# Local attention of a hybrid kernel: exponentials written back to the scores' PSUM bank and divided out of it, the statistics placed after the token shift has had time to land, and new instruction orders

## The reference

```python
def _layer(x, wqkv, qs, ksc, wo, lg, lb, w1, b1, w2, b2):
    h = shift_token(x)                 # half of the channels come from the token before
    q, k, v = split(h @ wqkv)          # 8 heads of 64
    q = l2norm(q) * qs; k = l2norm(k) * ksc
    q, k = rotary_xpos(q, k)
    o = local_attention(q, k, v)       # windows of 64 tokens, keys of this window and the one before
    x = x + o @ wo
    h = shift_token(x)
    h = layernorm(h) * lg + lb
    a, g = split(h @ w1 + b1)          # hidden width 341
    x = x + (a * gelu(g)) @ w2 + b2
# local_attention: attn = softmax(sim + mask); out = attn @ v
```

## Time and profile before

| | us |
|---|---|
| three runs, median (lowest to highest) | 2002.58 (1999.52 to 2009.76) |
| the profiled execution, own time | 2001.32 |
| its span | 1999.5 |
| PE, DVE, ACT, POOL busy in it | 1614.6, 1371.7, 1116.0, 453.6 |

### The profile page before, as it was taken

The page is one execution under the profiler, slowest core; times in us unless marked ns, Lnnn a source line. Parts: engine busy times, 40 slices in busy tenths (PEclk is TensorE's granted clock), DMA queues, the critical chain, the costliest instruction groups (busy, mean ns, idle before and its releaser), DMA issues.

```text
span 1999.5 us, 31315 instructions
## 1 busy us (share of the span) xinstructions
PE 1614.6 (81%) x9756; PEld 1271.6 (64%) x9787; DVE 1371.7 (69%) x3495; ACT 1116.0 (56%) x2975; POOL 453.6 (23%) x342
## 2 busy tenths in 40 slices
PE   6999989666466787888887899999967788888886
PEld 5888887344354565666666687777735666666665
DVE  4678768788956768677786466456656867768673
ACT  2354454332124777778777644434236777777774
POOL 1210010000003334343343100000023334334340
PEclk9999999676678999999999999989979999999998
DMA  4000000000010000000000000000000000000000
GB/s 136 1 1 0 0 0 1 0 1 0 0 53 1 3 3 1 3 2 3 3 1 3 2 1 0 0 0 0 1 0 3 2 3 1 3 3 2 3 1 24
DMA packets 15110, 13.49 MB, mean 7 GB/s; under 512 B 11286, under 2 KB 14266, under 8 KB 14650
## 3 DMA queue, kind: packets, MB, share of 16 engines
q1 hardware_dynamic: 15034, 12.55, 2.0%
HBM read 9.41 MB, written 1.05 MB: 5 GB/s over the span
## 4 chain that ended last, share of the span: by engine, by line
PE 50%; DVE 25%; issue 10%; ACT 7%; DMA 5%; SPq 1%; DVEq 1%; POOL 1%; ACTq 0%; POOLq 0%
DVE prob L1027 5%; DMA HS<-XH 5%; PE bank L1739 4%; PE bank L1680 4%; PE bank L1751 4%; PE bank L1700 3%; PE bank L1879 3%; DVE arena_ffn L984 3%; PE bank L1772 3%; DVE arena_ffn L980 2%; ACT prob L1437 2%; DVE nmaxF L717 2%; PE bank L1883 2%; PE bank L1691 2%; PE bank L1899 2%
## 5 line engine op out<-in xcount | busy, mean ns | idle before, releaser
L556 POOL TENSOR_TENSOR arena_ffn<-arena_ffn 128x1024 f32<-128x1024 f32 x60 | 140.9, 2348 | 434.2 <-DVE arena_ffn L984 434.2
L552 POOL TENSOR_TENSOR inv<-ssq,mhalf 128x16 f32<-128x16 f32 x64 | 188.3, 2942 | 160.6 <-DVE ssq L993 160.6
L1437 ACT ACTIVATE prob<-bank,nmaxF 128x128 f32<-128x128 f32 x512 | 180.9, 372 | 65.7 <-DVE nmaxF L717 65.7
L1751 PE MATMUL bank<-packF,hT 128*128 128x512 f32 x256 | 146.7, 702 | 74.6 <-DVE arena_ffn L984 66.4
L1027 DVE TENSOR_TENSOR prob<-prob,rdenF 128x512 f32<-128x512 f32 x128 | 180.2, 1408 | 4.4
L1714 PEld LDWEIGHTS bank<-arena_setup 128*128 128x128 f32 x1024 | 145.4, 205 | 18.5 <-issue 10.3
L1367 ACT ACTIVATE prob<-bank,nmax 128x128 f32<-128x128 f32 (+1 forms) x256 | 89.9, 420 | 118.3 <-DVE nmax L717 90.5
L1726 PE MATMUL bank<-ident,prob 128*128 128x128 f32 x512 | 83.5, 286 | 79.7 <-DVE prob L1027 79.7
L1714 PE MATMUL bank<-arena_setup 128*128 128x128 f32 x1024 | 143.9, 287 | 0.0
L540 POOL TENSOR_TENSOR rstd<-var,mhalf 128x2 f32<-128x2 f32 x24 | 17.0, 708 | 518.0 <-DVE var L679 518.0
L1726 PEld LDWEIGHTS bank<-ident,prob 128*128 128x128 f32 x512 | 57.1, 144 | 116.8 <-DVE prob L1027 110.0
(11 more groups left out here) (271 smaller groups left out, 4102.4 us busy)
## 6 DMA issues: line engine op xcount, KB each, us to landing
packF<-in_packF SPq DMA_DIRECT2D x1, 3122.0 KB
arena_history<-in_packG SPq DMA_DIRECT2D x1, 2560.0 KB, 9.8
HS<-XH SPq DMA_DIRECT2D x32, 63.5 KB
X<-in_x_tiled SPq DMA_DIRECT2D x1, 1024.0 KB, 5.0
out_dram<-X SPq DMA_DIRECT2D x8, 128.0 KB, 1.9
arena_setup<-in_const_masks_a SPq DMA_DIRECT2D x1, 512.0 KB, 5.5
HS<-XH SPq DMA_DIRECT2D x32, 0.2 KB
arena_setup<-in_const_rope SPq DMA_DIRECT2D x1, 256.0 KB
```

Source lines behind the costliest of these rows:

```text
L552: pool.tensor_tensor(inv[:, t, :, 0], ssq[:, t, :, 0], mhalf[:, 0:16], ALU.pow).then_inc(sems["inv_ready"], 1)
L556: pool.tensor_tensor(t1[:, t], t1[:, t], t2[:, t], ALU.add).then_inc(sems["rope_sum"], 1)
L1437: ins = act.activation(prob[:, u % 2, c * P:(c + 1) * P], bank[u % F_SCORE_BANKS][:, c * P:(c + 1) * P], ACT.Exp, bias=nmaxF[:, u, c:c + 1 ...
L1751: ins = pe.matmul(bank[banks[m]][:], hT[:, t * P:(t + 1) * P], f_at[f"wqkv{l}"][:, 512 * m:512 * m + 512], start=True, stop=True)
```

## The change

The exponentials are written over the scores in the PSUM bank, and the DVE multiplication reads that bank and writes `prob`. So `local_exp` no longer waits for the transposes of two units before (`pt_ready`); that wait is now `weigh`'s. `local_scores` waits until `weigh` of two units before (`norm_ready`) has read the bank, where it waited for the exponentials (`exp_ready`). The orders of DVE, ACT and PE in a window step are rewritten.

```diff
 # DVE, weigh(u)
                     dve.wait_ge(sems["exp_ready"], v.at("exp_ready", i, u + 1))
                     ch.link(dve.reciprocal(rdenF[:, u], denF[:, u]))
-                    pr = prob[:, u % 2].rearrange("p (c k) -> p c k", k=P)
-                    dve.tensor_tensor(pr, pr, rdenF[:, u].broadcast_to([P, 4, P]), ALU.mult).then_inc(sems["norm_ready"], 1)
+                    dve.wait_ge(sems["pt_ready"], v.at("pt_ready", i, u - 1))
+                    split = lambda a: a.rearrange("p (c k) -> p c k", k=P)
+                    dve.tensor_tensor(split(prob[:, u % 2]), split(bank[u % F_SCORE_BANKS][:]), rdenF[:, u].broadcast_to([P, 4, P]), ALU.mult).then_inc(sems["norm_ready"], 1)
 # DVE, win
+                attn_max(v, i, 0, 4, P, nmaxF, F_SCORE_BANKS)
                 scaled(v, i, 1)
+                if nxt:
+                    rope_part(vn, ni, nl, 0, 0)
+                attn_max(v, i, 1, 4, P, nmaxF, F_SCORE_BANKS)
+                if nxt:
+                    rope_part(vn, ni, nl, 0, 1)
                 if hid:
                     hidden_stats(*hid)
                 if nxt:
-                    rope_part(vn, ni, nl, 0, 0)
-                attn_max(v, i, 0, 4, P, nmaxF, F_SCORE_BANKS)
-                if nxt:
-                    rope_part(vn, ni, nl, 0, 1)
+                    norms(vn, ni, 0, sch)
+                weigh(0)
                 if m:
                     gated(*m)
-                weigh(0)
-                attn_max(v, i, 1, 4, P, nmaxF, F_SCORE_BANKS)
-                if nxt:
-                    norms(vn, ni, 0, sch)
+                weigh(1)
                 attn_max(v, i, 2, 4, P, nmaxF, F_SCORE_BANKS)
                 if nxt:
                     rope_part(vn, ni, nl, 1, 0)
-                weigh(1)
+                if m:
+                    mlp_end(m[0], m[1])
                 attn_max(v, i, 3, 4, P, nmaxF, F_SCORE_BANKS)
                 weigh(2)
-                if m:
-                    mlp_end(m[0], m[1])
...
+                local_residual(v, i, l)
                 if fin:
                     final_stats(m[0], m[1])
-                local_residual(v, i, l)
-                if fin:
                     norm_apply(m[0], m[1])
 # ACT, local_exp(u)
                 act.wait_ge(sems["max_ready"], v.at("max_ready", i, u + 1))
-                act.wait_ge(sems["pt_ready"], v.at("pt_ready", i, u - 1))
                 for c in range(4):
-                    ins = act.activation(prob[:, u % 2, c * P:(c + 1) * P], bank[u % F_SCORE_BANKS][:, c * P:(c + 1) * P],
-                                         ACT.Exp, bias=nmaxF[:, u, c:c + 1], accum_out=denF[:, u, c])
+                    cols = bank[u % F_SCORE_BANKS][:, c * P:(c + 1) * P]
+                    ins = act.activation(cols, cols, ACT.Exp, bias=nmaxF[:, u, c:c + 1], accum_out=denF[:, u, c])
 # ACT, win
                     shifted(vn, ni)
+                if m:
+                    prime(ACT.Gelu)
+                if nxt:
                     squares(vn, ni, 0)
                 if m:
-                    prime(ACT.Gelu)
                     gelus(*m)
                     prime(ACT.Exp, 1)
                 local_exp(v, i, 0)
                 take_qkT(v, i, 1)
+                local_exp(v, i, 1)
                 if nxt:
                     squares(vn, ni, 1)
-                local_exp(v, i, 1)
+                middle_values(v, i)
+                local_exp(v, i, 2)
                 probs_copy(v, i, 0)
-                local_exp(v, i, 2)
-                middle_values(v, i)
                 probs_copy(v, i, 1)
 # PE, local_scores(u)
-                pe.wait_ge(sems["exp_ready"], v.at("exp_ready", i, u - 1))
+                pe.wait_ge(sems["norm_ready"], v.at("norm_ready", i, u - 1))
 # PE, win
                     transpose_x(vn, ni, bank[2])
-                if m:
-                    hidden_gates(*m, 0)
+                local_scores(v, i, 0)
                 if nxt:
                     project_qk(vn, ni, nl, 0)
                 if m:
+                    hidden_gates(*m, 0)
                     pe.wait_ge(sems["down_used"], v.at("down_used", i, 0))
                     hidden_gates(*m, 1)
-                local_scores(v, i, 0)
                 local_scores(v, i, 1)
                 if m:
                     hidden_values(*m)
                 transpose_qk(v, i, 1)
                 if nxt:
                     project_qk(vn, ni, nl, 1)
+                transpose_probs(v, i, 0)
                 local_scores(v, i, 2)
-                transpose_probs(v, i, 0)
                 if m:
                     hidden_out(*m)
                 local_scores(v, i, 3)
+                transpose_probs(v, i, 1)
                 pe.wait_ge(sems["down_used"], v.at("down_used", i, 0))
                 weigh_values(v, i, 0)
-                transpose_probs(v, i, 1)
-                transpose_probs(v, i, 2)
...
                 weigh_values(v, i, 1)
+                transpose_probs(v, i, 2)
```

More of the change, by code:

```diff
@@ L1209, in setup_rest @@
                                                      f_at[f"b1_{l}"][0:n, c:c + 4:3], ALU.add))
-            credit(dve, "pt_copied", "o_used", "down_used", "phi_done", "lin_st", "lin_y")
+            credit(dve, "norm_ready", "pt_copied", "o_used", "down_used", "phi_done", "lin_st", "lin_y")
             for n, kind in enumerate(plan[1:], 1):
```

2 lines of the change are left out of this document (1 added, 1 removed).

## The result

The changed kernel takes 1897.19 us (median of four runs, 1894.08 to 1900.93) against 2003.38 for the kernel before; the ratio is 0.9468 with a 95% interval of 0.9437 to 0.9498. All ratios are of fast runs; one execution of e11, at 3913.43 us, was slow and stands in its median of ten but outside its ratio. The forecast was 1898. That number is closer than the reasons behind it: one wait was missing from the sum and other terms were too large or too small, and they cancel, which is luck.

What follows compares the result with a forecast made beforehand. No engine fills the 31.03 us step; a chain bounds it: residual and DMA 6.8, DVE 18.0, PE's tail 6.2. Savings of 87, 5, 7 and 5 make 104 us, so 1897 profiled, 1898 predicted; own range 1880 to 1915, wider 1866 to 1936.

Steps and rivals of the forecast that it cites:

- three signs of being wrong: L1089 or statistics stretched beside L556; L1437's mean moved over 0.05 us; PE idle over 2 us in an ordinary step.
- The multiplication out of PSUM: `weigh` on DVE takes 0.68 us, held by nothing, which removes 3.2 us of DVE work in an ordinary step.
- The cover for the shift: On DVE the token shift lands at 6.7 us, statistics start at 8.1 without a wait: 1.4 us of cover.
- The hold of the addition of epsilon: L1089 on DVE held by POOL's addition until 10.5 us; the sum left this out, with statistics ending at 9.2.
- The sum: Ordinary periods 87 us, final norm 5, second steps 7, first and last steps 5: 104 us saved, giving 1898.
- a rival with 10%: Statistics held: L1089 waits for POOL's addition, `norms` and `weigh(0)` come 1.3 us later, 35 us in all, 1933; 10%.
- The walk's 26.3 us: Ordinary step followed instruction by instruction in the new orders: transposes 3 start at 20.1 us, plus PE's tail of 6.2.
- the 0.5 added to it: The same walk over the old order gave 30.5 against the trace's 31.03, so 0.5 us was added, making 26.9.
- the exponentials' price: Extra time per ACT exponential into PSUM: taken as 0, bounds -0.02 and +0.05 us; the skill pointed below zero.
- ACT ends last: In the ordinary step's second half ACT, not DVE, ends last, with exponentials 3 done at 18.8 us.
- The final norm's statistics: Behind the residual, POOL's power and copy come late, adding 2.7 us: 30.3 against 31.3 us in 5 periods.
- Second steps of the groups: Two steps without MLP, each 3.5 us shorter: 7 us of the total.

Runs made afterwards that it cites:

- e11: Data path of e4 with DVE's new order alone, PE, ACT and POOL in old orders: 1997.44 us, ratio 0.9923.
- e7: e3 with epsilon added by e2's reduction (new orders, exponentials into SBUF): 1911.3 us, ratio 0.9511.
- e2: Changed kernel with the scalar operation that adds epsilon made a reduction over variance and an epsilon column: 1840.19 us, ratio 0.9172.
- e5: Changed kernel with the statistics ahead of the second part of the first rotation on DVE: 1884.8 us, ratio 0.937.
- e3: Changed kernel with the old data path (exponentials into SBUF, multiplied there), new orders kept: 1986.63 us, ratio 0.989.
- e9: Changed kernel with one extra ACT copy (0.63 us) in each step: 1900.68 us.
- e8: Changed kernel with the edits of e1 and e2, plus one extra ACT copy (0.63 us) in each step: 1846.69 us.
- e10: Changed kernel with the edits of e1 and e2, and the two middle-value copies moved from ACT to DVE: 1834.99 us, ratio 0.9123.
- e1: Changed kernel with the final statistics ahead of the residual again in steps with a final norm: 1876.57 us, ratio 0.9352.
- e4: New data path alone (exponentials to PSUM, multiplied out of it) in the old orders of the kernel before: 1987.01 us, ratio 0.9911.

## Why the prediction was right, and where it was not

**Its own signs.** The prediction named three signs of being wrong, and two of them came: the addition of epsilon (L1089) is stretched beside POOL's addition, and PE is idle over 2 us in an ordinary step (2.71). The third, L1437's mean off by over 0.05 us, did not (372 to 340 ns). The number 1898 came out all the same, by luck.

**The multiplication out of PSUM** was right: 690 to 693 ns, 128 of 128. e7 against e2 gives the worth of the data path in the new orders, with the addition of epsilon held in neither: 71 us.

**The cover for the shift** was right: DVE is not idle before the statistics. With the statistics one part of the rotation earlier (e5), DVE waits 0.18 us and the shift has landed 6.8 us into the step; in the changed kernel the statistics start at 7.8. The cover is 1.0 us, not 1.4.

**The hold of the addition of epsilon** was the step that failed. The sum took 0.17 us for it and left the rest to a rival with 10%; it takes 1.58 us. The rival had place and mechanism (1.3 us later for `norms` and `weigh(0)`) but not the size, 35 us. e2 shows 57, since the longer wait of PE also comes with a stretch at half clock in every third ordinary period, and since the periods with a final norm have the hold too. In e2 and e5, where no single wait of PE in an ordinary period is over 1.7 us, no ordinary period has such a stretch. The rule of the Trainium skill (SBUF — State Buffer, Who interferes with whom) named the instruction, and that the reduction is free of it; e2, e3 and e5 agree with it, 1575 against 157 ns in the median, and I gave it too small a chance. I also read it wrongly for `norms`, which I called free: its reduction is, but its clamp (L993) is a scalar operation, and in e5 that is the one held, 1.30 us. What the trace had, L1096 at 711 ns, was already one such case: in the kernel before it ran from 1985.26 to 1985.97, and a POOL addition (L565) from 1985.20 to 1985.92.

**The walk's 26.3 us and the 0.5 added to it** were too long for a kernel without the hold: e2, which is that kernel, has 25.6. The 0.5 was not there. Of the other 0.7, up to 0.5 can be the exponentials, 0.03 us cheaper than the walk's (339 against 368 ns in the median) and 16 in ACT's row; no run changes their price alone, so this share is an estimate. The Trainium skill (ScalarE: Activation LUTs, Step-by-step) had the sign of the exponentials' price right. So the forecast of a step was 1.3 us too long and the hold made the step 1.3 us longer. They cancel, and 26.9 came out for the wrong reason.

**ACT ends last** was wrong for the changed kernel, where the chain goes over the hold, `weigh(0)` and PE, and an added ACT copy is covered (e9). It was half right with the hold gone: the chain of e2 does go over ACT, but PE ends within some tenths of a us of it (e8, e10).

**The final norm's statistics** were right in place: PE is idle for 2.65 us, forecast as 2.7. The gain was not there: I took 30.3 us a period, and the four have 31.0, 30.9, 30.8 and 32.8, together 125.5 us against 125.1 before. e1 gives what the new place costs: 16.6 us in these four periods, 20.6 between medians.

**The sum** cancels once more. There are 22 ordinary periods in the trace, not 21. They were 31.27 us in the mean and not 31.03, since some had a stretch at half clock before as well, and they are 27.32, not 26.9: 3.95 us each and not 4.15, and 87 us in all, as forecast. The final norm brings nothing where the sum had 5. Second steps of the groups (30.5 and 31.6 us, now 26.2 and 26.6) bring 9.4 where it had 7, and last steps (27.2 and 28.5, now 23.9 and 22.3) another 9.4. With 4.1 us before the first shift and 1.8 lost outside the groups that is 107.6 us between the profiled spans, where the sum had 104.

**Not foreseen at all** was that the halves are worth so little apart (e3, e4, e11), and the reasons differ. The new orders alone (e3) bring the hold of the addition of epsilon, 75 us of it (e7). The data path alone (e4) has no such hold, but of the multiplication's 3.2 us, which I had put down as taken off the chain, 2 come back as waits for the bank. Why the stretches at half clock fall in every third period was not tested.

## What to carry to other kernels

When a wait on a shared resource is taken from one instruction, look at what stands beside the other party afterwards: here the hold moved from a 512-element multiplication to a two-element addition, then (e5) to the next small instruction. An order that makes a small result late for another engine's list (here a power that stands on POOL ahead of the next copy) makes everything behind it in that list late as well, 4.2 us a period here. And a number that comes out right is no proof of its terms: only the runs that took one term away, and the count of the periods by kind, showed that errors had cancelled.

## What the runs showed of the hardware

A scalar operation of DVE on 128x2 values, issued while a POOL addition of 128x1024 ran, ended with that addition (1575 ns against 169 in the median; 760.69 and 760.67 us in the step read), while a reduction of 128x4 to 128x2 in the same place took 157 ns, and the multiplication with one operand in PSUM 691 ns (at 770.10, beside the addition at 770.06). Batch-norm statistics beside the same addition kept their 0.21 us. An exponential of 128x128 took 339 ns with its output in PSUM and 365 to 368 ns in SBUF. Steps of TensorE with one wait of 2.71 us had, in every third ordinary period, a stretch at half clock that made them 1.3 us longer (the changed kernel); with 2.64 us in two pieces (e5), or with 1.36 us (e2), no ordinary period had one.
